# Image 0's softmax rows for tile 0 spread by TensorE instead of DMA, with the opening of a 32-image attention kernel reordered around it

## What is computed

```python
xt = gn(x).reshape(b, c, n).transpose(0, 2, 1)
w = einsum('bnc,oc->bno', xt, qkv_w)             # then split in 12 heads of 32
w_normed = w / max(sqrt(sum(w*w over n)), 1e-12)
Pi = softmax(sum(w_normed**2 over d) * temp, over the heads)
Pi_n = Pi / (sum(Pi over n) + 1e-8)
attn = 1 / (1 + sum(Pi_n * w*w over n))          # one number for each head and channel
out = -(w * Pi) * attn
y = x + einsum('bnc,oc->bno', out, out_w) + out_b
```

## Time and profile before

| | us |
|---|---|
| median of 3 runs (873.52 to 873.78) | 873.63 |
| the profiled execution | 873.38 |
| its span | 871.5 |

### The profile page before, as it was taken

One profiled execution on the slowest core, in us unless ns is written; L12 is line 12 of the kernel. 1 busy time (PEld: TensorE's weight loads), 2 busy tenths in 40 slices (PEclk: granted clock), 3 DMA queues, 4 the chain that ended last, 5 costly groups with the idle time before them and its releaser, 6 DMA issues.

```text
span 871.5 us, 14048 instructions
## 1 busy us (share of the span) xinstructions
PE 855.4 (98%) x4322; PEld 682.3 (78%) x4322; DVE 748.8 (86%) x1389; ACT 526.5 (60%) x676; POOL 230.9 (26%) x105
## 2 busy tenths in 40 slices
PE   7989999999999999999999999999999999999996
PEld 6767788777788777788777788777788777788785
DVE  7799889899888889889889889888989889889667
ACT  4667556667555667556667556667556667556531
POOL 2432123332123332123332123331123332123300
PEclk9999999999999999999999999999999999999999
DMA  7324564634664544564544664544564534564423
GB/s 279 129 90 152 224 227 154 220 133 174 223 225 160 201 151 169 223 227 171 197 142 171 224 225 174 195 139 172 224 226 175 195 134 177 223 225 155 149 78 145
DMA packets 45523, 158.53 MB, mean 182 GB/s; under 512 B 20130, under 2 KB 24226, under 8 KB 37538
## 3 DMA queue, kind: packets, MB, share of 16 engines
q1 hardware_dynamic: 37264, 155.47, 48.5%
q10 hardware_dynamic: 8210, 2.59, 1.2%
HBM read 105.56 MB, written 52.49 MB: 181 GB/s over the span
## 4 chain that ended last, share of the span: by engine, by line
PE 95%; DVE 3%; issue 1%; DMA 1%; ACT 0%; DVEq 0%; ACTq 0%
PE acc L580 89%; PE scores L672 5%; DVE WS L884 1%; DMA bias<-in_L_conv_out_b 1%; DVE WV L928 0%; PE acc L563 0%; DVE UL L957 0%; ACT UH L438 0%; DVE W1L L741 0%; DVE stats L767 0%; PE acc L557 0%; DVE dots L923 0%; DVE dots L925 0%; DVE dots L921 0%; PE small L574 0%
## 5 line engine op out<-in xcount | busy, mean ns | idle before, releaser
L378 POOL TENSOR_TENSOR XL<-XN,XH 128x1024 fp32r<-128x1024 f32 x93 | 222.5, 2409 | 574.3 <-ACT XH L476 548.0
L448 ACT ACTIVATE WS<-acc 128x1024 f32<-128x1024 f32 x96 | 98.4, 1025 | 246.2 <-PE acc L580 183.5
L580 PE MATMUL acc<-UH,W2H 128*128 128x512 f32 x576 | 178.3, 391 | 2.8 <-ACT UH L438 2.8
L580 PE MATMUL acc<-XH,W1H 128*128 128x512 f32 x576 | 178.4, 391 | 0.2 <-DVE W1L L741 0.2
L580 PE MATMUL acc<-XH,W1L 128*128 128x512 f32 x576 | 177.7, 390 | 0.0
L580 PE MATMUL acc<-UH,W2L 128*128 128x512 f32 x576 | 177.6, 390 | 0.0
L965 DVE SCALAR_TENSOR_TENSOR X<-acc,bias,X 128x1024 f32<-128x1024 f32 x95 | 119.0, 1277 | 38.6 <-PE acc L580 38.4
L580 PE MATMUL acc<-UL,W2H 128*128 128x512 f32 x576 | 149.9, 396 | 0.8 <-DVE UL L957 0.8
L580 PE MATMUL acc<-XL,W1H 128*128 128x512 f32 x576 | 146.3, 390 | 0.0
L580 PEld LDWEIGHTS acc<-UL,W2H 128*128 128x128 f32 x576 | 105.5, 188 | 34.7 <-issue 12.3
L438 ACT ACTIVATE UH<-WV 128x1024 fp32r<-128x1024 f32 x96 | 98.2, 1056 | 52.8 <-DVE WV L910 33.1
(11 more groups left out here) (88 smaller groups left out, 457.3 us busy)
## 6 DMA issues: line engine op xcount, KB each, us to landing
PIB<-pi SPq DMA_DIRECT2D x96, 528.0 KB, 5.2
X<-in_x SPq DMA_DIRECT2D x31, 1536.0 KB, 6.3
out_y<-X SPq DMA_DIRECT2D x31, 1536.0 KB, 6.3
gathered<-stats_rows ACTq DMA_DIRECT2D x28, 72.0 KB, 5.2
pi<-PIT SPq DMA_DIRECT2D x96, 16.5 KB
X<-in_x SPq DMA_DIRECT2D x3, 512.0 KB, 4.7
out_y<-X SPq DMA_DIRECT2D x2, 512.0 KB, 2.7
WV<-in_L_conv_qkv_w SPq DMA_DIRECT2D x1, 576.0 KB, 6.6
```

What stands on the lines that cost most here:

```text
L378: pool.tensor_tensor(XL[:, t, :], XN[:, t, :], XH[:, t, :].bitcast(F32), ALU.subtract).then_inc(xl_done, 1)
L448: act.activation(square_tile(i, t), acc[:, t, :], ACT.Square, accum_out=sumsq[:, t:t + 1]).then_inc(squared, 1)
L580: last = pe.matmul(out[:, h * BANK:(h + 1) * BANK], w[:, k, m * P:(m + 1) * P], r[:, k, h * BANK:(h + 1) * BANK], start=(n == 0 and k == 0 ...
```

## The change

For image 0 alone, tile 0's softmax rows no longer go through DRAM. DVE writes the first four heads' softmax into a small tile, ScalarE widens it to 32 channels per head into the (still unused) square tile of image 1, TensorE turns it with eight transposes into PSUM (`scores` and `small`, now one allocation), ScalarE copies that once to get the sum over positions, and `attend_tile(FIRST, 0)` reads the rows from PSUM. SyncE's queue writes and reads two tiles of image 0 instead of three.

Beside that: image 0 is loaded in six pieces of 128x512, each with its semaphore; XH's tile 0 of image 0 is made by halves, and the first product takes its first input tile half by half; two of the six first idle turns and the eight ahead of `head_sums(1)` are gone; `product_by_k(FIRST)` stands directly behind image 1's first product, with `head_sums(1)` inside it after k = 0 and its lower terms ordered by k; image 1's variances, image 2's means and variances move to other places among the terms. DVE takes over XN of tiles 0 and 1 and the keeping of W of tiles 0 and 1 of image 1 from ScalarE; image 2's statistics are split; image 3's all come after `finish(FIRST, 1)`.

```diff
-IDLE_TURNS = (6, 4, 8, 15)
+IDLE_TURNS = (4, 4, 15)
...
-        scores = pb("scores", [P, BANK])
+        spread_ps = pb("spread_ps", [P, 2, BANK])
+        scores = spread_ps[:, 1]
...
-            for t in range(T):
-                sp.dma_start(x_tile(FIRST, t), FIRST.of(x_img)[:, t * N:(t + 1) * N]).then_inc(first_loaded[t], 16)
+            for k in range(T * HALVES):
+                columns = slice(k * BANK, (k + 1) * BANK)
+                sp.dma_start(X[:, FIRST.slot, columns], FIRST.of(x_img)[:, columns]).then_inc(first_loaded[k], 16)
...
-                    for t in range(T):
+                    tiles = range(1 if by_pe(j) else 0, T)
...
+            def widen_heads(j):
+
+                act.wait_ge(heads_kept, pe_spread(j))
+                if j.follows(1):
+                    act.wait_ge(u_step, (j - 1).counts(U_STEPS, 1))
+                act.activation(wide_heads(j).rearrange("p (b d h) -> p b d h", b=BLOCKS, d=D),
+                               pi_heads[:].unsqueeze(2).to_broadcast([P, BLOCKS, D, HPT]), ACT.Copy)\
+                    .then_inc(heads_widened, 1)
...
+            def totals(j):
+
+                act.wait_ge(rows_spread, 1)
+                act.activation(square_tile(j + 1, 1), spread_ps[:].rearrange("p k n -> p (k n)"), ACT.Copy,
+                               accum_out=pi_tot[:, 0:1]).then_inc(totals_kept, 1)
...
                 square_w(zero, 1)
                 square_w(zero, 2)
                 keep_w(zero, 1)
-                normalise(one, 0)
                 keep_w(zero, 2)
+                act.wait_ge(xn_done, one.counts(T, T - 1))
+                normalise(one, T - 1)
                 exponentials(zero)
-                normalise(one, 1)
-                normalise(one, 2)
+                widen_heads(zero)
+                totals(zero)
+                u_hi(zero, 0)
+                act.wait_ge(w_kept, one.counts(T, 1))
                 square_w(one, 0)
+                act.wait_ge(w_kept, one.counts(T, 2))
+                square_w(one, 1)
                 group_seeds(two)
-                keep_w(one, 0)
-                square_w(one, 1)
                 square_w(one, 2)
-                keep_w(one, 1)
-                normalise(two, 0)
-                u_hi(zero, 0)
                 keep_w(one, 2)
-                x_hi(two, 0)
                 u_hi(zero, 1)
                 u_hi(zero, 2)
                 exponentials(one)
-                for t in range(1, T):
+                for t in range(T):
                     normalise(two, t)
                     x_hi(two, t)
 
+            def x_hi_half():
+
+                rstd_0, shift_0 = norm_of(FIRST)
+                act.wait_ge(gn_step, GN_STEPS)
+                act.activation(XH[:, 0, 0:BANK], x_tile(FIRST, 0)[:, 0:BANK], ACT.Identity, bias=shift_0,
+                               scale=rstd_0).then_inc(first_half, 1)
+                act.activation(XH[:, 0, BANK:N], x_tile(FIRST, 0)[:, BANK:N], ACT.Identity, bias=shift_0,
+                               scale=rstd_0).then_inc(xh_done, 1)
+
             w1_higher()
-            for t in range(T):
+            x_hi_half()
...
+                        if not i.follows(1) and (t, ns, k) == (0, (0, 1), 0):
+                            pe.wait_ge(first_half, 1)
+                            for h in range(HALVES):
+                                if h == 1:
+                                    pe.wait_ge(xh_done, 1)
+                                for w in (W1H, W1L):
+                                    pe.matmul(acc[:, 0, h * BANK:(h + 1) * BANK], w[:, 0, 0:P],
+                                              XH[:, 0, h * BANK:(h + 1) * BANK], start=(w is W1H), stop=False)
+                            continue
...
+                    if k == 0 and not j.follows(1):
+                        head_sums(j + 1)
+                lower = [(t, k) for t in range(T) for k in range(T)]
+                for t, k in lower if j.follows(1) else sorted(lower, key=lambda tk: tk[1]):
+                    if t == 0:
+                        pe.wait_ge(ul_done[k], j.counts(1, 1))
+                    last = term(acc[:, t, :], t, (W2H, W2L), (UH, UL), 2, k)
+                    if k == T - 1:
+                        last.then_inc(m2_done, 1)
...
+            def spread_heads(j):
+
+                pe.wait_ge(heads_widened, pe_spread(j))
+                pe.wait_ge(sm_step, j.counts(SM_STEPS, SM_STEPS))
+                for b in range(BLOCKS):
+                    last = pe.transpose(spread_ps[:].rearrange("p k n -> p (k n)")[:, b * P:(b + 1) * P],
+                                        wide_heads(j)[:, b * P:(b + 1) * P], identity[:])
+                last.then_inc(rows_spread, 1)
...
-                             (2, hi, 2): [lambda: group_variances(FIRST + 1)]})
+                             (2, hi, 1): [lambda: group_variances(FIRST + 1)]})
             opening_product(FIRST + 1, [(0, hi), (1, hi), (2, hi), (0, lo), (1, lo), (2, lo)],
                             {(0, hi, 1): [lambda: head_sums(FIRST)],
-                             (0, lo, 1): [lambda: group_means(FIRST + 2)],
-                             (1, lo, 0): [lambda: group_variances(FIRST + 2)]})
-            pe.wait_ge(gn_step, (FIRST + 2).counts(GN_STEPS, GN_AGGREGATED))
-            idle_turns(small[:, P:2 * P], IDLE_TURNS[2])
-            head_sums(FIRST + 1)
+                             (1, hi, 2): [lambda: spread_heads(FIRST)],
+                             (1, lo, 0): [lambda: pe.wait_ge(tile_step, tile_steps(FIRST, 0, TILE_STEPS)),
+                                          lambda: group_means(FIRST + 2)],
+                             (2, lo, 1): [lambda: group_variances(FIRST + 2)]})
...
+            def keep_w(i, t):
+
+                dve.wait_ge(m1_done, i.counts(T, t + 1))
+                dve.wait_ge(w2_lo, T)
+                dve.tensor_copy(w_tile(i, t), acc[:, t, :]).then_inc(w_kept, 1)
...
+                if by_pe(j):
+                    dve.tensor_tensor(pi_heads[:], EX[:, :, 0:HPT],
+                                      srec[:].unsqueeze(2).to_broadcast([P, BLOCKS, HPT]), ALU.mult).then_inc(heads_kept, 1)
...
+                if t == 0 and by_pe(j):
+                    rows = spread_ps[:].rearrange("p k (b n) -> p (k b) n", n=QUAD)
+                    dve.wait_ge(rows_spread, pe_spread(j))
+                    dve.wait_ge(squared, j.counts(T, t + 1))
+                    dve.wait_ge(totals_kept, 1)
+                    dve.tensor_tensor_reduce(in_blocks(square_tile(j, t)), rows, in_blocks(square_tile(j, t)), 1.0, 0.0,
+                                             ALU.mult, ALU.add, dot_t).then_inc(u_step, 1)
+                    dve.memset(wait_cell[:], 0.0).then_inc(tile_step, 1)
+                else:
+                    rows = PIB[:, t, :, 0:QUAD]
+                    dot(j, t)
+                    dve.tensor_reduce(total, PIB[:, t, :, QUAD], AX_X, ALU.add).then_inc(tile_step, 1)
+                for other in within:
+                    other()
                 dve.wait_ge(tile_step, base + 1)
                 dve.wait_ge(u_step, j.counts(U_STEPS, t + 1))
...
+            dve.wait_ge(mm_gn, one.counts(MM_VARIANCES, MM_AGGREGATED))
+            group_stats(two, [0])
+            part_spreads(one)
             dve.wait_ge(temp_kept, 2)
             dve.tensor_tensor(head_temp[:], head_mask[:], temp_o[:].unsqueeze(2).to_broadcast([P, T, QUAD]),
                               ALU.mult).then_inc(temp_kept, 1)
-            part_spreads(one)
             moments_kept(one)
             group_norm(one)
             for t in range(T):
                 x_hi(one, t)
             head_sum_weights(FIRST)
+            normalise(one, 0)
+            normalise(one, 1)
             softmax_shift(FIRST)
             softmax_divide(FIRST)
-            group_stats(two, range(T))
+            group_stats(two, [1, 2])
             part_moments(two)
+            attend_tile(FIRST, 0)
+            keep_w(one, 0)
             dve.wait_ge(mm_gn, two.counts(MM_VARIANCES, MM_AGGREGATED))
-            group_stats(three, [0])
             part_spreads(two)
-            moments_kept(two)
-            group_stats(three, [1])
-            group_norm(two)
-            attend_tile(FIRST, 0)
+            keep_w(one, 1)
+            attend_tile(FIRST, 1, [lambda: moments_kept(two)])
             head_sum_weights(one)
-            attend_tile(FIRST, 1)
             attend_tile(FIRST, 2)
             dve.memset(wait_cell[:], 0.0).then_inc(u_step, U_STEPS - T)
             softmax_shift(one)
+            group_norm(two)
             softmax_divide(one)
             for t in range(T):
                 u_lo(FIRST, t)
             finish(FIRST, 0)
             finish(FIRST, 1)
-            group_stats(three, [2])
+            group_stats(three, range(T))
```

More of the change, by code:

```diff
@@ L152, in conv_attention @@
         srec = sb("srec", [P, BLOCKS])
+        pi_heads = sb("pi_heads", [P, BLOCKS, HPT])
         PIT = sb("PIT", [P, T, QUAD + 1])
```

(32 more changed lines are left out.)

24 lines of the change are left out of this document (16 added, 8 removed).

## The result

| | before | after |
|---|---|---|
| median (lowest to highest) | 873.70 (873.26 to 874.19) | 876.74 (875.62 to 878.38) |
| ratio to before, 95% interval | | 1.0036 [1.0024, 1.0048] |
| profiled execution, its span | 873.38, 871.5 | 875.62, 873.8 |

The account below looks back on a forecast made before the run. TensorE, busy 98%, bounds the kernel, so only stalls ahead of the loop can be saved. +0.4 at image 2's head sums and -0.5 from the front gave -0.1: 873.3 profiled, 873.5 median, range 871.7 to 875.2.

Parts of the forecast that it names:

- The front: Opening up to the first product: start 0.95 earlier, of which 0.5 counts because the slow clock halves it.
- The first product starts 0.95 earlier: TensorE's opening: two idle turns fewer bring the start from 14.24 to 13.3.
- in six pieces the statistics end up to 0.65 earlier: DVE's opening statistics of image 0: gain of one instruction, 3.89 / 6, making room for the earlier mean.
- The lower bound (0.4 late): First product's start if all three more load issues, 0.43 each, delayed the first weights: 0.4 late.
- The middle: Image 2's statistics to image 0's product end: new stall until about 48.5, then product over at 60.6 instead of 63.30.
- UL comes in time (DVE is through with it at 58.1): Image 0's second product: TensorE runs through from 48.5 to 59.65 without waiting for UL.
- The stretch from finish to the head sums: DVE's queue from image 0's first finish to image 2's head sums: 4.95 + 2.43 + 11.1 + 0.72, ending at 78.85.
- rival 1: TensorE keeps its gain: DVE's stretch from finish to head-sum weights takes some 16 us, not 19.2; 870.9; chance 0.13.
- After that it runs through again: Loop after image 2's head sums: TensorE without waits, DVE having some 3.5 us to spare per image.
- Rival 2 (the clock rises later): TensorE's first product: clock rise at 19.6 or later; with 20.1 the time is 875.5; chance 0.12.
- the rise hardly wanders from run to run: Clock rise in the first product, about 15.9: taken as steady since three runs of before agree within 0.26 us.
- The range: Whole kernel's time: 871.7 to 875.2, with no more than 0.2 left out.

Follow-up runs that it names:

- before_six_loads: Kernel before with image 0 in six loads and four first idle turns, without the halves of XH; 873.57, ratio 1.0001.
- pool_waits: Changed kernel with POOL's wait for the last UL of image 0 moved ahead of image 2's first XL; 876.44, ratio 1.0034.
- both: Changed kernel with POOL's wait moved ahead of image 2's first XL and four of image 3's six statistics ahead of finish; 873.55, ratio 1.0000.
- after_equal: Changed kernel with tile 0's two counters brought up by 16 once at the start; 875.72, ratio 1.0026.
- all_mended: Changed kernel with POOL's wait ahead of image 2's first XL, four statistics ahead of finish, equal counters and image 0 in three loads; 872.79, ratio 0.9990.
- before_shifted: Kernel before with 128 bytes left unused ahead of PIT and PIB; 873.64.
- equal_stats: Changed kernel with equal counters and four of image 3's six statistics ahead of finish; 875.74, ratio 1.0024.
- stats_ahead: Changed kernel with four of image 3's six statistics moved ahead of the first finish of image 0; 876.03, ratio 1.0030.

## Why the prediction was wrong

- **The front: wrong.** "The first product starts 0.95 earlier", 13.3; it was 14.47. The step that failed is "in six pieces the statistics end up to 0.65 earlier": they ended 0.5 later, because the pieces landed later, and the mean follows them and not the turns. The lower bound (0.4 late) held, by luck: it was made of the weights' issues, and the delay came from the statistics. The forecast charged the three more issues to the weights alone, but they stand ahead of X's own last pieces too; that this is why the pieces land late is likely and not shown. That the six loads are behind it is borne out by `before_six_loads`, where the statistics end 0.7 later, but both kinds wander: 8.4 to 8.7 in the six profiles with three loads, 8.5 to 9.6 in the eleven with six.
- **The middle: right, but for UL.** Copies at 1.2 (1.22), reads from PSUM as dear as from SBUF (the dot 1.23), TensorE waiting near 48.5 (48.78). The step that failed is "UL comes in time (DVE is through with it at 58.1)": DVE was through at 60.5. POOL was met only as "XL of image 1 starts earlier"; that image 2's first XL, kept clear of the UL only by its early start, would now run beside it was not looked at. Of the 1.7 by which finish began behind the forecast (61.33 against 59.65), 1.1 is the collision (`pool_waits`: 60.21), 0.3 the late copy at 48.78, and 0.3 small slips. The late copy is the opening's delay carried on: image 0's head sums start at 31.31 where they started at 31.01 before.
- **The stretch from finish to the head sums: right.** Forecast 19.2, measured 80.27 - 61.33 = 18.9. So rival 1 fails for the reason given, and `both` shows that the statistics were as dear as said: with four of them ahead of finish the stretch is 2.3 shorter (2.43 forecast). With the front's 0.5 not gained, the 1.7 of the middle and 0.3 back from here, the 1.9 between the forecast head sums (78.35) and the measured are told.
- **"After that it runs through again": wrong.** The waits on `pi_written` were seen as counts and not as instructions. DVE does have time to spare, as argued; what has none is the chain from the rows to PIB. By the profile that costs 0.4, by the median of `after_equal` 1.0.
- **Rival 2 (the clock rises later): not this.** The product's first four matmuls were slow again, until about 15.8, as before. That this is the lower level is read from their length alone (0.44 against 0.23); the granted clock of the profile reads 1.00 over this stretch in both kernels. And "the rise hardly wanders from run to run" is wrong: in `all_mended` the first matmuls were fast from 14.21 on, in `before_shifted`, whose opening is the kernel before's, from 14.03 on, and so in six of the seventeen profiles. What sets it no run here tells.
- **The range** took its width from unknown prices in known steps and left nothing for a step not seen.

What stays open: the profile of the change loses 0.4 in its loop, its median some 0.8 more; that the rest is more late head sums of the same kind is likely, from the scatter that goes with the counters, but no trace shows those runs, and the fall of the clock at the kernel's end, 0.7 in seven of the seventeen profiles, scatters the runs too. Why the pieces land late was not tried apart from their number, and the worth of three loads is not settled.

## What to carry to other kernels

If an order of work was made by a wait at one spot, list which instructions it kept apart by time alone: a step that moves may put the two side by side without any wait changing. Keep counters that are waited on together at the same value, even at the price of an idle increment: an exception for one image at the start is paid for all through the loop. And a mend that gains less than its trace shows points to a second cause behind it.

## What the runs showed of the hardware

- XL on POOL and UL on DVE, both float32 with two inputs in SBUF, held each other up, each until the other's instruction was over: 3.43 for 1.22, and 3.19 for 2.41.
- The granted clock falls after TensorE's waits, but not always: after 1.99 in `equal_stats`, not after 1.98 at the same place in `stats_ahead`. At the end of the kernel TensorE waits 2.28 or 2.29 in every profile; in ten of the seventeen the clock stays at 1.00, in seven it falls. From image 31's head sums to the end that takes 34.7 to 34.8 us in the ten and 35.4 to 35.5 in the seven. Here before and `all_mended`, the wait and the stretch behind it (granted clock 1.00 and 0.60):

```profile
853.68 0.73 PE L580 MATMUL acc<-UH,W2H 128*128 128x512 f32 x2 [2.28 <-ACT UH L438]
```
```profile
854.00:858.00 4.00, 3.81 (x17) 2.84 (x16) 3.76 (x10) 1.06 (x1) 0.00 (x0) 1.00 0.02 8
```
```profile
852.30 0.73 PE L629 MATMUL acc<-UH,W2H 128*128 128x512 f32 x2 [2.29 <-ACT UH L463]
```
```profile
854.00:858.00 4.00, 4.00 (x12) 3.10 (x12) 3.86 (x9) 1.52 (x2) 0.00 (x0) 0.60 0.00 0
```

- One more value among the waits ahead of DVE's copy into PIT cost 0.22 us of idle time in each image that had it.
- With three loads of 512 KB the statistics ended at 8.4 to 8.7 us (six profiles), with six of 256 KB at 8.5 to 9.6 (eleven).
